# Row sums by VectorE instead of a TensorE product, and a new order, in a fused stack of four graph layers

## What is computed

```python
x = layernorm(x + where(mask, relu((x + A^T x) @ W1 + b1) @ W2 + b2, 0))      # layer 0
degree = A.sum(axis=-1)
x = layernorm(x + relu(concat([x, (A^T x) / degree]) @ W^T + b))              # layer 1
d = (A + I).sum(axis=-1) ** -0.5
x = layernorm(x + d * ((A + I) @ (d * (x @ W))) + bias)                       # layer 2
h = relu(x @ W1a (rows i) + x @ W1b (rows j) + b1)                            # layer 3
out = sum over j of A[i, j] * (layernorm(h @ W2 + b2) * gamma + beta)
x = layernorm(x + out)
```

## Time and profile before

| | |
|---|---|
| median of 3 runs | 449.63 us (449.41 to 449.93) |
| the profiled execution | 449.61 us, its span 447.9 us |
| busy: PE | 429.5 us (96%) |
| busy: DVE | 422.7 us (94%) |
| busy: ACT | 393.8 us (88%) |
| busy: POOL | 353.6 us (79%) |

### The profile page before, as it was taken

The page is one execution under the profiler, slowest core; times in us unless marked ns, Lnnn a source line. Parts: engine busy times, 40 slices in busy tenths (PEclk is TensorE's granted clock), DMA queues, the critical chain, the costliest instruction groups (busy, mean ns, idle before and its releaser), DMA issues. The chain is left out here.

```text
span 447.9 us, 14059 instructions
## 1 busy us (share of the span) xinstructions
PE 429.5 (96%) x3391; PEld 403.8 (90%) x3391; DVE 422.7 (94%) x1555; ACT 393.8 (88%) x1001; POOL 353.6 (79%) x651
## 2 busy tenths in 40 slices
PE   7599989999999999999999999999999999999993
PEld 3599989999999999898999999999999999999992
DVE  6999999999999999998999999999999999999976
ACT  2378979999999899979899999999999999999994
POOL 3569979999999899953776878787878787878772
PEclk9989999999999999999999999999999999999998
DMA  6134334445444743232422223222323232323111
GB/s 225 43 86 124 101 127 159 154 157 159 155 157 152 240 162 120 80 129 78 136 89 73 88 66 92 66 92 64 94 64 94 64 94 63 95 65 97 59 37 50
DMA packets 50939, 47.60 MB, mean 106 GB/s; under 512 B 5584, under 2 KB 42576, under 8 KB 50896
## 3 DMA queue, kind: packets, MB, share of 16 engines
q1 hardware_dynamic: 49760, 46.45, 33.7%
q10 hardware_dynamic: 1136, 0.66, 0.5%
HBM read 28.22 MB, written 18.87 MB: 105 GB/s over the span
## 5 line engine op out<-in xcount | busy, mean ns | idle before, releaser
L1621 PE MATMUL bank<-w2c,hE 128*128 128x128 f32 x512 | 68.3, 277 | 0.4 <-ACT bank L928 0.4
L1621 PEld LDWEIGHTS bank<-w2c,hE 128*128 128x128 f32 x512 | 63.5, 192 | 2.6 <-issue 0.7
L1289 DVE TENSOR_TENSOR ym<-bank,wE 128x512 f32<-128x512 f32 x64 | 43.4, 684 | 4.3 <-POOL wE L775 3.3
L1264 DVE TENSOR_REDUCE ssum<-sqE 128x4 f32<-128x512 f32 x63 | 42.7, 678 | 3.0 <-ACT sqE L945 2.7
L1122 DVE BATCH_NORM_STATS2 stats<-t 128x6 f32<-128x128 f32 x192 | 44.5, 273 | 1.0 <-issue 1.0
L945 ACT ACTIVATE sqE<-bank 128x512 f32<-128x512 f32 x63 | 38.0, 603 | 8.0 <-PE bank L1621 8.0
L915 ACT ACTIVATE hE<-bank,front 128x512 f32<-128x512 f32 x64 | 43.5, 680 | 1.5 <-PE bank L1601 1.5
L742 POOL TENSOR_TENSOR half<-ym 128x512 f32<-128x512 f32 x31 | 39.6, 1276 | 5.7 <-DVE ym L1289 2.1
L775 POOL TENSOR_TENSOR wE<-erstd,fits 128x12 f32<-128x12 f32 x31 | 6.6, 213 | 44.8 <-DVE erstd L1278 44.8
L726 POOL TENSOR_TENSOR gHl<-gH,gHu 128x512 fp32r<-128x512 f32 x32 | 40.8, 1276 | 1.2 <-ACT gHu L899 1.2
L928 ACT ACTIVATE bank<-b2c 128x512 f32<-128x512 f32 x62 | 37.4, 604 | 0.5 <-DVE ym L1289 0.4
(11 more groups left out here) (192 smaller groups left out, 1643.6 us busy)
## 6 DMA issues: line engine op xcount, KB each, us to landing
hh_scratch<-hh SPq DMA_DIRECT2D x32, 256.0 KB, 2.2
gH<-hh_scratch SPq DMA_DIRECT2D x32, 256.0 KB, 2.7
A<-adj_groups SPq DMA_DIRECT2D x32, 128.0 KB, 2.1
res_scratch<-res SPq DMA_DIRECT2D x32, 128.0 KB, 2.0
gRES<-res_scratch SPq DMA_DIRECT2D x32, 128.0 KB, 2.0
AT<-adjT_groups SPq DMA_DIRECT2D x31, 128.0 KB, 2.2
out<-y SPq DMA_DIRECT2D x30, 128.0 KB, 1.8
X<-x_groups SPq DMA_DIRECT2D x29, 128.0 KB, 2.2
```

The source lines that it names most:

```text
L1264: nc.vector.tensor_reduce(ssum[q][:, g * ELL:(g + 1) * ELL], sqE[g][:, :, :], AX.X, ALU.add).then_inc(b[f"ssE{g}_ready"], 1)
L1289: nc.vector.tensor_tensor(ym[q][:, g, :, :], YE_ps[g], spread_last(wE[q][:, g * ELL:(g + 1) * ELL]), ALU.mult).then_inc(b[f"ymE{g}_ready"], 1)
L1621: last = nc.tensor.matmul(ps[:, i, :], hidden[:, i * P:(i + 1) * P], w2c[:, :], start=False, stop=i == tiles - 1, skip_group_check=seeded)
```

## The change

Each degree is now a row sum of `A`, taken by VectorE in one reduction per group (`sum_rows`). ScalarE makes degree times beta by scaling the row of beta with the degree, once per graph (`spread_degrees`). The product `count_row`, its copy `keep_sums` and the matrix `beta1` go. `find_holes` and `keep_counts` become one VectorE stage of two instructions, and `negate_mean` and `make_shift` one VectorE instruction. The transposed adjacency's load no longer waits for the product; the adjacency's load waits for the row sum as well. Every moment of `dense_stages`, `T3` and `FIRST` is set anew.

```diff
-        beta1 = sb("beta1", [P, P + 1])
-        mean1 = [sb(f"mean1_{k}", [P, GROUP]) for k in K4]
-        sums = sb("sums", [P, SLOTS, GROUP, P + 1])
-        bdeg, deg = sums[:, :, :, 0:P], sums[:, :, :, P]
+        bdeg = sb("bdeg", [P, SLOTS, GROUP, P])
+        deg = sb("deg", [P, SLOTS, GROUP])
...
             def next_at(k, r, n):
-                    sp.wait_ge(s["sums_psum"], n)
...
             def next_a(k, r, n):
                     sp.wait_ge(s["xT_psum"], n)
+                    sp.wait_ge(s["deg_ready"], n)
...
-            def find_holes(k, r, n):            # GpSimd
-                nc.gpsimd.tensor_scalar(hole[:, k, :], deg[:, k, :], -1.0, None, ALU.is_equal).then_inc(s["hole_found"], 1)
-            def keep_counts(k, r, n):
-            def negate_mean(k, r, n):
-            def make_shift(k, r, n):
-                nc.gpsimd.tensor_tensor(shift1[k][:, :], mean1[k][:, :], rstd[1][k][:, :], ALU.mult).then_inc(s["shift1"], 1)
...
-            def keep_sums(k, r, n):             # ScalarE
-                act.wait_ge(s["sums_psum"], n)
-                nc.scalar.activation(sums[:, k, :, :], sums_ps, ACT.Copy).then_inc(s["sums_ready"], 1)
+            def spread_degrees(k, r, n):
+                wait_past(act, s["res_ready"], n - SLOTS)
+                act.wait_ge(s["deg_ready"], n)
+                for g in range(GROUP):
+                    last = nc.scalar.activation(bdeg[:, k, g, :], C["beta"], ACT.Copy, scale=deg[:, k, g:g + 1])
+                last.then_inc(s["bdeg_ready"], 1)
...
+                def ln_shift(k, r, n):          # VectorE
+                    dve.wait_ge(s[f"rstd{layer}"], n)
+                    wait_past(dve, s[f"x{layer + 1}_ready"], n - SLOTS)
+                    nc.vector.scalar_tensor_tensor(shift1[k][:, :], mv[layer][k][:, :, 0], -1.0, rstd[layer][k][:, :], ALU.mult, ALU.mult).then_inc(s["shift1"], 1)
+            def sum_rows(k, r, n):
+                dve.wait_ge(a_loaded[k], 16 * r + 16)
+                wait_past(dve, s["bdeg_ready"], n - SLOTS)
+                wait_past(dve, s["found_ready"], n - SLOTS)
+                nc.vector.tensor_reduce(deg[:, k, :], A[k][:, :, :], AX.X, ALU.add).then_inc(s["deg_ready"], 1)
+            def find_holes(k, r, n):
+                dve.wait_ge(s["deg_ready"], n)
+                wait_past(dve, s["dis_ready"], n - SLOTS)
+                nc.vector.tensor_scalar(hole[:, k, :], deg[:, k, :], -1.0, None, ALU.is_equal)
+                nc.vector.scalar_tensor_tensor(found[:, bass.ds(SLOTS * r + k, 1), :].rearrange("p o c -> p (o c)"), deg[:, k, :], -1.0, deg[:, k, :],
+                                               ALU.is_equal, ALU.add).then_inc(s["found_ready"], 1)
...
-            def count_row(k, r, n):             # TensorE
-                    last = nc.tensor.matmul(sums_ps[:, g, :], AT[k][:, g, :], beta1[:, :], start=True, stop=True)
...
-            dense_stages = [(5.48, find_flaws), (14.94, sum0), (15.62, stats0), (16.57, var0), (19.4, rstd0), (20.43, apply0), (26.49, degrees), (27.21, sum1a),
+            dense_stages = [(10.53, find_flaws), (12.97, sum0), (14.66, stats0), (15.07, var0), (16.48, rstd0), (18.17, apply0), (21.6, sum_rows), (22.47, degrees), (22.54, find_holes), (26.9, sum1a),
```

More of the change, by code:

```diff
@@ new lines, in gnn_stack @@
+        FIRST = {("Qp", 0): 218.78, ("Qp", 1): 221.25, ("Qp", 2): 227.9, ("Qp", 3): 239.8, ("Qp", 4): 253.32, ("Qp", 5): 267.61, ("Qp", 6): 306.85,
[7 rows of a table added]
+                 ("app", 0): 262.32, ("app", 1): 305.2, ("app", 2): 319.87, ("app", 3): 361.77, ("app", 4): 371.01, ("app", 5): 387.17,
+                 ("app", 6): 422.19, ("app", 7): 436.06, ("beg", 0): 219.96, ("beg", 1): 224.02, ("beg", 2): 228.68, ("beg", 3): 239.93,
+                 ("beg", 4): 259.37, ("beg", 5): 296.92, ("beg", 6): 313.98, ("beg", 7): 440.09, ("cols", 0): 224.22, ("cols", 1): 231.86,
+                 ("cols", 2): 244.99, ("cols", 3): 265.18, ("cols", 4): 269.98, ("cols", 5): 273.19, ("cols", 6): 295.88, ("cols", 7): 346.64,
[4 rows of a table added]
+                 ("frec", 3): 351.2, ("frec", 4): 382.52, ("frec", 5): 441.45, ("frec", 6): 490.69, ("frec", 7): 602.77, ("fstd", 0): 250.02,
+                 ("fstd", 1): 265.15, ("fstd", 2): 310.5, ("fstd", 3): 314.45, ("fstd", 4): 349.23, ("fstd", 5): 374.56, ("fstd", 6): 376.19,
[6 rows of a table added]
+                 ("idx", 0): 201.95, ("idx", 1): 219.68, ("idx", 2): 224.94, ("idx", 3): 232.42, ("idx", 4): 239.27, ("idx", 5): 261.41,
+                 ("idx", 6): 309.91, ("idx", 7): 323.33, ("kS", 0): 220.1, ("kS", 1): 225.27, ("kS", 2): 232.24, ("kS", 3): 249.27,
+                 ("kS", 4): 260.55, ("kS", 5): 272.48, ("kS", 6): 319.75, ("kS", 7): 462.87, ("kST", 0): 223.74, ("kST", 1): 230.76,
+                 ("kST", 2): 245.75, ("kST", 3): 252.39, ("kST", 4): 266.44, ("kST", 5): 272.67, ("kST", 6): 292.67, ("kST", 7): 342.05,
[8 rows of a table added]
+                 ("rec", 0): 232.95, ("rec", 1): 244.22, ("rec", 2): 253.62, ("rec", 3): 274.16, ("rec", 4): 274.19, ("rec", 5): 394.11,
+                 ("rec", 6): 396.49, ("rec", 7): 418.45, ("rows", 0): 220.56, ("rows", 1): 226.17, ("rows", 2): 233.27, ("rows", 3): 259.47,
+                 ("rows", 4): 288.99, ("rows", 5): 314.01, ("rows", 6): 349.94, ("rows", 7): 350.23, ("rs", 0): 241.92, ("rs", 1): 252.28,
[8 rows of a table added]
+                 ("sh", 7): 363.46, ("spl", 0): 211.88, ("spl", 1): 218.85, ("spl", 2): 228.3, ("spl", 3): 229.67, ("spl", 4): 263.04,
+                 ("spl", 5): 294.24, ("spl", 6): 334.12, ("spl", 7): 385.66, ("spu", 0): 167.83, ("spu", 1): 214.69, ("spu", 2): 225.88,
+                 ("spu", 3): 232.17, ("spu", 4): 245.91, ("spu", 5): 264.69, ("spu", 6): 270.35, ("spu", 7): 300.76, ("sqc", 0): 230.56,
+                 ("sqc", 1): 234.8, ("sqc", 2): 246.35, ("sqc", 3): 258.44, ("sqc", 4): 275.42, ("sqc", 5): 305.65, ("sqc", 6): 306.46,
+                 ("sqc", 7): 371.98, ("st", 0): 252.62, ("st", 1): 273.31, ("st", 2): 280.01, ("st", 3): 328.61, ("st", 4): 338.96,
+                 ("st", 5): 368.78, ("st", 6): 388.28, ("st", 7): 419.76, ("std", 0): 231.48, ("std", 1): 240.1, ("std", 2): 249.9,
+                 ("std", 3): 262.33, ("std", 4): 306.49, ("std", 5): 307.85, ("std", 6): 314.13, ("std", 7): 332.02, ("tot", 0): 247.36,
+                 ("tot", 1): 259.67, ("tot", 2): 284.51, ("tot", 3): 291.93, ("tot", 4): 331.08, ("tot", 5): 331.52, ("tot", 6): 347.55,
[5 rows of a table added]
@@ L589, in store @@
                 sp.dma_start(out_d[bass.ds(u * GROUP, GROUP), :, :].rearrange("g p f -> p g f"), (gRES if at_end(u) else y4)[q][:, :, :]).then_inc(out_stored[q], 16)
-            dense_stages = [(24.2, next_a), (25.28, next_x), (25.66, next_at), (26.27, keep(ot, ot_s, "ot_ready", ot_stored)),
-                     (58.51, keep(res, res_s, "res_ready", stored)), (69.62, keep(hh, hh_s, "hh_ready", stored))]
+            dense_stages = [(27.18, next_a), (20.2, next_x), (32.13, next_at), (22.65, keep(ot, ot_s, "ot_ready", ot_stored)),
+                     (63.46, keep(res, res_s, "res_ready", stored)), (68.08, keep(hh, hh_s, "hh_ready", stored))]
             edge_stages = [(("idx", 0.5), next_ot), (("spl", "hs", 1.5), next_h), (("rs", 0.8), next_res), (("app", 1), store)]
@@ L681, in mark_edges @@
                 nc.gpsimd.tensor_tensor(ot[k][:, :, :], AT[k][:, :, :], spread_rows(ident[:, :]), ALU.subtract).then_inc(s["ot_ready"], 1)
-            def find_holes(k, r, n):
-                pool.wait_ge(s_setp, 3)
-                pool.wait_ge(s["sums_ready"], n)
-                nc.gpsimd.tensor_scalar(hole[:, k, :], deg[:, k, :], -1.0, None, ALU.is_equal).then_inc(s["hole_found"], 1)
-            def keep_counts(k, r, n):
-                pool.wait_ge(s["hole_found"], n)
-                nc.gpsimd.tensor_tensor(found[:, bass.ds(SLOTS * r + k, 1), :].rearrange("p o c -> p (o c)"), deg[:, k, :], hole[:, k, :], ALU.add).then_inc(s["found_ready"], 1)
             def guard_root(k, r, n):
@@ L1115, in _ @@
             dve.wait_ge(s_const, 16)
-            nc.vector.tensor_copy(beta1[:, 0:P], C["beta"])
             def layer_norm(layer):
@@ L1193, in sum2 @@
                 last.then_inc(s["t2_done"], 1)
-            stats0, var0, rstd0, apply0 = layer_norm(0)
-            stats1, var1, rstd1, _ = layer_norm(1)
-            stats2, var2, rstd2, _ = layer_norm(2)
+            stats0, var0, rstd0, apply0, _ = layer_norm(0)
+            stats1, var1, rstd1, _, make_shift = layer_norm(1)
+            stats2, var2, rstd2, _, _ = layer_norm(2)
             def cast_counts():
@@ L1481, in mlp0a @@
                     keep_busy(bank[7], 2 - k)
-            def count_row(k, r, n):
-                wait_past(pe, s["sums_ready"], n - 1)
-                pe.wait_ge(at_loaded[k], 16 * r + 16)
-                for g in range(GROUP):
-                    last = nc.tensor.matmul(sums_ps[:, g, :], AT[k][:, g, :], beta1[:, :], start=True, stop=True)
```

(4 more changed lines are left out.)

67 lines of the change are left out of this document (18 added, 49 removed), and 84 rows, old and new, of tables (FIRST, T3).

## The result

The kernel after takes 481.52 us (median of 4 runs, 479.93 to 482.65), the kernel before 449.70 beside it: a ratio of 1.0705, interval 1.0670 to 1.0741. The forecast was 454.4 with a range from 445 to 466. The direction was right, the size was not, and the time lies outside the range. Of the kernels further down, one (hs_turn) had an execution of 849.06 us among four, which stands apart from the others (466.95 to 468.67) and is not in its ratio.

A forecast was written before the change was run, and what follows sets the result against it. DVE was to become the dense phase's bound at 5.62 us a group against 5.42: 24 spacings give +4.8 us on the profiled 449.61, all else at no cost, so 454.4 us, range 445 to 466.

The forecast's parts named there:

- the new order of the edge phase, since PE is busy there all the time with the same instructions: Edge phase: reordering counted at no cost, 1.5 us either way if PE waits or its start is better.
- PE's gaps in the edge phase: Edge phase: named as a sign of being wrong that would put the difference into the new order there.
- The late groups and the passage: Last groups: counted at no cost, since their DVE work lies in the passage beside 3.6 free us.
- DVE's 3.6 free us of 20: Passage: DVE's free time read from the busy rows, taken to absorb the late groups' DVE work.
- No slower stretch after 85: Dense phase: sign of being right, spacing near 5.6 from 35 us on with no slower stretch after 85 us.
- the 5.42: Dense phase before the change: mean spacing per group, 130.04 / 24 us, which the new spacing has to beat.
- DVE as the bound near 5.62: Dense phase: DVE's 5.14 us of work plus 0.48 held up sets the spacing; likeliest case, chance 0.41.
- The 0.48: Dense phase: us per group POOL holds DVE up, the old 0.59 times POOL's busy share, 4.55 of some 5.6.
- PE's 0.44 is given away: Dense phase: the product's 0.44 us per group saved on PE gains nothing, because DVE becomes the bound.
- PE's relief: Rival, dense phase: DVE held up 0.15 us or less, spacing 5.29, 446.5 us (442.9 with nothing held up); chance 0.33.
- The small ones held up: Rival, dense phase: holes and shift each held up 0.32 us by POOL, spacing 6.26, 469.8 us; chance 0.17.
- The early part: First four groups: PE's earlier inputs against 0.53 us more per group on DVE, between -1 and +2 us; counted at no cost.

The follow-up runs named there:

- hs_turn: turn_both with GpSimd's add_ends (`hs`) set back behind split_lower: 468.10 us, ratio 1.0426.
- t3_back: Kernel after with the old order of the edge phase (old table T3, all 49 moments): 468.24 us, ratio 1.0427.
- hs_turn2: hs_turn with VectorE's loop over the units beginning behind yC (turn -1.6): 463.41 us, ratio 1.0339.
- turn_both: Kernel after, same order, with VectorE's loops over the units (turn -4.6) and the dense rounds (turn -4.2) begun elsewhere: 471.21 us, ratio 1.0508.
- product_kept: Kernel after with TensorE's old product per graph put back beside the row sums, its result unused: 480.25 us, ratio 1.0693.
- gap2: Kernel after with sum1b and then apply0 placed ahead of inverse_root on VectorE, where GpSimd waits: 481.16 us, ratio 1.0735.
- work_only: The change's operations in the order of the kernel before in all phases, only new instructions given own places: 479.44 us, ratio 1.0678.
- hs_back: Kernel after with one edge-phase moment set back, GpSimd's add_ends (`hs`) behind split_lower again: 488.30 us, ratio 1.0863.

## Why the prediction was wrong

- **The step that failed** is "the new order of the edge phase, since PE is busy there all the time with the same instructions", at no cost, 1.5 us either way. It measured 12.2 us in the 24 units, and t3_back got 13.3 back with the passage; the sign that the prediction had named for it, PE's gaps in the edge phase, is there. PE full in the old order says nothing of the new one: its inputs came late, by `hs` and by the place of DVE's loop beginning, and hs_turn2 gives it all back.
- **The late groups and the passage**, counted at no cost, failed with it: +3.1 for the last four groups, whose `z` came every 5.1 to 5.75 us against 4.0 to 5.6 before, and +2.4 behind them. DVE's 3.6 free us of 20 were read at 200 to 220 us, behind these groups, whose last `z` in the kernel before starts at 188.04.
- **"No slower stretch after 85"** was wrong: the dense loop's beginnings, 4.8 us by turn_both. The prediction read the 5.42 as a mean and did not look at what stands at a loop's beginning in the new order.
- **DVE as the bound near 5.62** was right in mechanism, and off by 0.13: 5.21 of work against 5.14, and 0.54 held up (5.75 - 5.21) against 0.48. Without the loop's beginnings (three of 1.5 us) that is 24 x 0.33 = 7.9 us, against the forecast 4.8. The 0.48 came from the old hold times a busy share, which no run shows as a rule: the same work was held up for more or less in each order that was tried. "PE's 0.44 is given away" was right, by product_kept.
- **The rivals.** PE's relief did not come through (product_kept costs nothing). The small ones held up: hardly in after, where `hole` takes 0.16, `found` 0.15 and `shift` 0.22 (0.14 alone), but in gap2 `hole` was held up for 0.43 us in the mean. So the price was real, and the order decides who pays it.
- **The early part** came within its bounds, -0.1 by `z`. By `rdeg` it would seem 2.8 us shorter, but only because the new order takes the reciprocal earlier in a group's turn; in work_only, with the same row sums in the old order, the fourth `rdeg` starts at 36.05, no earlier than before.

## What to carry to other kernels

An engine that is 100% busy in the old order is no reason to cost a new order at nothing: go through the new list for what each of its inputs waits for, and look at what stands at each loop's beginning, where an engine needs over 1 us of queued work, none of it waiting, to cover the arithmetic. Taking work off one engine pays only if the engine that gets the rest has room in the same stretch; shorten the one and restore the other, and two runs say which of them is the bound. When two orders are compared stretch by stretch, a border must be an instruction that has kept its place in both. Where two engines hold each other up, a hold that is pushed off one instruction returns at the next that comes beside a running one; count it per turn, in the spacing, not per instruction.

## What the runs showed of the hardware that was not expected

- A loop's beginning on VectorE took 1.35 to 1.45 us of register arithmetic in the edge phase, with that of `begun`, and 1.5 in the dense phase. Behind four queued instructions it cost nothing, behind one it cost 0.4 to 0.7 us of idle time, and what came late could then be held up by GpSimd, as `begun` in hs_back. The Trainium skill, "Advanced Engine Details and Errata", Engine Queue Depths, gives VectorE a queue of eight; the rows show four in use, which does not speak against it.
- A VectorE instruction on two columns can wait as long as a large one: `hole` 0.58 us in the mean of gap2 and 0.69 in a turn where it met `xb`, 0.15 alone.
- The prediction saw `apply0` wait 0.32 of the 0.54 us that POOL's instruction had left. `sum1b` at 75.82 waited 0.92 - 0.40 = 0.52 of the 0.63 that `res` had left, and in gap2 `hole` ended 0.02 to 0.03 us behind `xb`, whether 0.67, 0.50 or 0.31 us of it were left (at 130.44, 76.95 and 71.05). That is near to the rule of the Trainium skill, "SBUF — State Buffer", Who interferes with whom, that the later one waits for the whole of the first.
